# Where eight units of the shared expert run: ahead of the experts' loop, between the gate and table steps, in place of five

## The reference, cut to what matters

```
xf = layernorm(x)                                  # 2048 tokens x 512
scores = softmax(xf @ gate_w.T); topk_w, topk_idx = top_k(scores, 6)     # 64 experts
buf_tok[e, 0:128] = the first 128 tokens that chose expert e, in order   # buf_w: their weights
for each expert e:
    gu  = xf[buf_tok[e]] @ gate_up_proj[e]         # 128 x 512 @ 512 x 384
    hid = silu(gu[:, :192]) * gu[:, 192:]
    routed[buf_tok[e]] += (hid @ down_proj[e]) * buf_w[e]
shared = (silu(xf @ shared_gate_w.T) * (xf @ shared_up_w.T)) @ shared_down_w.T   # 384 wide
return x + routed + shared
```

## Time and profile before

| what | value |
|---|---|
| median of three runs | 596.72 us |
| the profiled execution: time, span | 597.44 us, 595.6 us |
| PE busy | 539.4 us, 91% of the span |
| DVE, ACT, POOL busy | 246.1, 161.7, 225.1 us |
| chain that ended last, by engine | PE 76%, DVE 11%, DMA 5%, issue 4% |
| its largest lines | L852 29%, L711 11%, L722 7%, L837 6% |
| mean granted TensorE clock | 0.974 |
| bytes moved | 155.05 MB, mean 260 GB/s |

### The profile page before, as it was taken

One profiled execution on the slowest core, in us unless ns is written; L12 is line 12 of the kernel. 1 busy time (PEld: TensorE's weight loads), 2 busy tenths in 40 slices (PEclk: granted clock), 3 DMA queues, 4 the chain that ended last, 5 costly groups with the idle time before them and its releaser, 6 DMA issues.

```text
span 595.6 us, 6264 instructions
## 1 busy us (share of the span) xinstructions
PE 539.4 (91%) x2087; PEld 291.8 (49%) x2087; DVE 246.1 (41%) x641; ACT 161.7 (27%) x342; POOL 225.1 (38%) x221
## 2 busy tenths in 40 slices
PE   5999996676799999999999999999999999999490
PEld 2555543343355555555555555555555555554130
DVE  1885979999223222222123223222222223223473
ACT  4767787662111111211111111212111111210000
POOL 3052246632523543444334543444344434412300
PEclk9999999987999999999999999999999999999796
DMA  8956478795458999899988999999999999785486
GB/s 288 338 208 235 113 255 278 245 390 205 124 198 276 298 298 298 289 305 280 278 271 267 295 327 306 281 267 292 268 289 307 295 291 288 180 249 119 51 316 255
DMA packets 53559, 155.05 MB, mean 260 GB/s; under 512 B 7248, under 2 KB 8784, under 8 KB 51856
## 3 DMA queue, kind: packets, MB, share of 16 engines
q1 hardware_dynamic: 34800, 109.74, 50.8%
q0 software_dynamic: 16320, 40.39, 29.6%
q10 hardware_dynamic: 2400, 4.46, 2.2%
HBM read 116.28 MB, written 38.28 MB: 260 GB/s over the span
## 4 chain that ended last, share of the span: by engine, by line
PE 76%; DVE 11%; DMA 5%; issue 4%; ACT 2%; POOL 1%; DVEq 0%; SPq 0%; POOLq 0%; ACTq 0%
PE bank L852 29%; PE bank L711 11%; PE bank L722 7%; PE bank L837 6%; PE bank L811 5%; PE bank L827 5%; PE bank L834 5%; PE bank L624 5%; DMA out<-y,table 3%; PE bank L612 2%; PE bank L818 2%; DVE x L1109 1%; DVE bn L1112 1%; DMA w<-in_W 1%; DVE ones_hi L1174 1%
## 5 line engine op out<-in xcount | busy, mean ns | idle before, releaser
L852 PE MATMUL bank<-gu_w,gxT 128*128 128x384 f32 x512 | 178.9, 493 | 2.2 <-ACT gxT L1040 1.4
L547 POOL DMA_INDIRECT out<-y,table x35 | 55.8, 1593 | 213.4 <-DVE y L1337 194.6
L852 PEld LDWEIGHTS bank<-gu_w,gxT 128*128 128x128 f32 x512 | 93.3, 190 | 79.7 <-issue 28.8
L1048 ACT ACTIVATE eg<-bank 128x192 f32<-128x192 f32 x64 | 21.2, 332 | 287.6 <-PE bank L852 284.6
L711 PE MATMUL bank<-xnT,upT 128*128 128x512 f32 x192 | 90.5, 617 | 8.5 <-DVE shid L1214 8.5
L1323 DVE TENSOR_TENSOR hid<-bank,eg 128x192 f32<-128x192 f32 x64 | 22.9, 358 | 179.7 <-ACT eg L1048 164.1
L553 POOL DMA_INDIRECT gx<-rows_dram,table x64 | 63.3, 989 | 28.2 <-issue 19.2
L1337 DVE TENSOR_SCALAR y<-bank,gx 128x512 f32<-128x512 f32 x64 | 45.1, 746 | 60.3 <-PE bank L837 60.3
L711 PEld LDWEIGHTS bank<-xnT,upT 128*128 128x128 f32 x192 | 36.3, 198 | 47.2 <-issue 37.9
L624 PE MATMUL bank<-w,h1T 128*128 128x512 f32 x128 | 57.7, 593 | 0.0
L547 POOL DMA_INDIRECT odd_sum<-y,table x29 | 45.9, 1584 | 8.9 <-issue 8.9
(11 more groups left out here) (179 smaller groups left out, 512.8 us busy)
## 6 DMA issues: line engine op xcount, KB each, us to landing
gu_w<-in_gate_up SPq DMA_DIRECT2D x64, 768.0 KB, 6.5
dn_w<-in_down SPq DMA_DIRECT2D x32, 768.0 KB
x<-in_x SPq DMA_DIRECT2D x4, 1024.0 KB, 13.0
feat_dram<-feat SPq DMA_DIRECT2D x16, 256.0 KB, 4.0
out<-shid SPq DMA_DIRECT2D x8, 512.0 KB
odd_sum<-shid SPq DMA_DIRECT2D x8, 512.0 KB
rows_dram<-rows ACTq DMA_DIRECT2D x4, 1024.0 KB, 6.4
gu_w<-out SPq DMA_DIRECT2D x4, 1024.0 KB, 7.9
```

The lines of the kernel that those rows point to most:

```text
L547: pool.indirect_dma_start(sums[lane(e)], bass.IndirectOffsetOnAxis(ap=table[:, e:e + 1], axis=0), y[:, e % YB, :], None, compute_op=ALU.ad ...
L852: last = nc.tensor.matmul(GU[e % 2][:, 0:2 * I], gxT[:, e % 2, c, :], gu_w[:, e % U, c, :], start=(c == 0), stop=(c == KC - 1))
```

## The change

`EARLY` goes from 5 to 8, so the loop holds 24 units in place of 27, spread over the same experts by the same formula. Ahead of the loop PE's order has units 0 to 5 each one place earlier or in a new place: unit 0 between the turns of tiles 5 and 6, unit 1 behind the logits of batch 1, unit 2 behind those of batch 2, unit 3 behind `invert_rest`, unit 4 between the last `place` and the third `invert`, unit 5 behind the first `collect`, and units 6 and 7 (the first two `shared_down`) behind the second. ACT's `silu` and DVE's `shared_up` steps move with them, and DVE adds the results of units 6 and 7 to `x` behind the last table step. One further line, in the general path that this execution doesn't enter, has another constant.

```diff
-EARLY = 5
+EARLY = 8
@@ PE
+                unit(0)
                 xn_turn(6)
                 xn_turn(7)
                 place(0)
                 gate(1)
                 turn_logits(1)
-                unit(0)
+                unit(1)
...
                 turn_logits(2)
-                unit(1)
+                unit(2)
                 invert(0)
...
                 invert_rest()
-                unit(2)
+                unit(3)
                 place(3)
+                unit(4)
                 invert(2)
                 pe.wait_ge(cross2_ready, 1)
                 collect(RFIN, cross2, k.pick_z, lambda lo_: lo_).then_inc(spare_done, 1)
-                unit(3)
+                unit(5)
                 invert(3)
                 pe.wait_ge(cross_ready, 1)
                 collect(LIST, cross, k.pick_a, lambda lo_: SLO - 1 - lo_).then_inc(fin_done, 1)
-                for u in range(4, EARLY):
+                for u in range(6, EARLY):
                     unit(u)
@@ ACT
                 gate_exp(1)
+                copy_logits(2)
                 silu(0, 0)
-                copy_logits(2)
                 store_rows(2)
...
                     copy_xn(3 * TB + t)
+                silu(0, 1)
                 gate_exp(2)
                 copy_logits(3)
                 store_rows(3)
                 gate_exp(3)
-                silu(0, 1)
@@ DVE
                 split_low(1)
+                shared_up(0, 0)
                 split_rest()
-                shared_up(0, 0)
                 choose(3)
...
                 cross_of(cross2, RTB, cross2_ready)
+                shared_up(0, 1)
                 split_high(3)
                 split_low(3)
                 dve.wait_ge(spare_done, 1)
                 nc.vector.tensor_copy(spare[:], POS[:, RFIN])
-                shared_up(0, 1)
+                shared_up(0, 2)
                 dve.wait_ge(tbl_done, B)
                 cross_of(cross, TBL, cross_ready)
...
                 link(nc.vector.tensor_tensor(gap[:], top[:, :, 0], top[:, :, 1], ALU.subtract))
+                for u in range(2 * SC, EARLY):
+                    shared_down(u - 2 * SC)
@@ general path
-            stage(vector=lambda: nc.vector.tensor_scalar(fits[:], bank[2][:, 0:E], SHI - 0.5, None, ALU.is_lt))
+            stage(vector=lambda: nc.vector.tensor_scalar(fits[:], bank[2][:, 0:E], SHI - 0.5 - AWAY, None, ALU.is_lt))
```

## The result

| | before | after |
|---|---|---|
| median (lowest to highest) of four runs each | 597.05 us (596.23 to 599.62) | 588.43 us (588.27 to 589.87) |
| the profiled execution: time, span | 597.44, 595.6 us | 588.57, 587.0 us |
| mean granted TensorE clock | 0.974 | 0.980 |
| PE busy | 539.4 us | 537.9 us |

The ratio is 0.9856, with a 95% interval of 0.983 to 0.9882: 8.6 us less, where 9.3 were forecast. PE's busy time hardly moves, since the units aren't fewer; they only stand where PE idled.

The account below looks back on a forecast made before the run. PE was taken to bound the loop, and DVE's tables the part ahead of it. Saving 8.6 us in the loop and 0.7 ahead gave 9.3 us off the 596.72 median: 587.4 us, range 585.8 to 591.0.

Parts of the forecast that it names:

- The loop follows PE: In the loop, a unit costs its full PE time, so moving three out saves 8.60 us (bounds 0 to 8.60).
- the loop isn't shorter: Rival, 7%: loads or scatters pace the loop, PE idles in the units' place, only 0.7 us stays: 596.0 us.
- my argument on the loads: In the loop, weights are asked for 23 us ahead and the slowest landing took 14.9 us, so loads keep up.
- Ahead of the loop: Before the loop, the last `invert` starts at 149.5 instead of 150.27: 0.7 us gained, bounds 0 and 0.8.
- The step on unit 5: Behind the first `collect`, unit 5 ends at 147.9 to 149.3, ahead of DVE's tables at 149.5, which alone hold `invert`.
- Unit 2: Behind batch 2's logits, waits for the silu ending near 118.1, ends at 121.6, before the first `invert` at 122.30; cost 0.
- the cover gone: Ahead of the first `invert`, without its idle time unit 2 would delay only turns that have slack of their own.
- Units 6 and 7: Behind the second `collect`, need 5.16 of the 5.2 us before the gather's rows: 0 if they fit, at worst 4.4 late.
- The clock rival: Rival, 12%: the clock falls just ahead of units 6 and 7, which end late: 589.0 to 590.5 us.
- its two prices: Units 6 and 7 end 3.1 us late (590.5 us) after a 6.8 us half-clock stretch, 1.6 late (589.0) after half that.
- The factor 1.85: Slowdown of a unit at the lower clock, from 6.35 us against 3.44 at the full clock, used in the late-end prices.
- everything from there on only moves earlier: From expert 58's scatter at 530.89 to the kernel's end, all steps only start earlier, so the loop's saving is kept.

Follow-up runs that it names:

- e7: Changed kernel with its 24 loop units packed one to an expert from expert 2 on, experts 26 to 63 having none: 593.22 us, ratio 0.992.
- e3: Changed kernel with two further `shared_down` (units 8 and 9) moved from the loop to behind the second `collect`: 588.88 us, ratio 0.9864.
- e5: Changed kernel with units 6 and 7 back in the loop and six matmuls whose results nobody reads in their place: 594.56 us, ratio 0.9953.
- e8: Changed kernel with DVE's last `shared_up` step, behind the loop, put ahead of the wait for the last scatters: 588.5 us, ratio 0.9843.
- e6: Changed kernel with ACT's first silu ahead of the copy of batch 2's logits again, as in the kernel before: 588.1 us, ratio 0.9836.
- e2: Changed kernel with units 6 and 7 back in the loop and units 0 to 5 left ahead of it: 596.14 us, ratio 0.998.
- e1: Changed kernel with units 5, 6 and 7 back in the loop, keeping the new order of units 0 to 4: 599.71 us, ratio 1.0042.

## Why the prediction was right, point by point

**The loop follows PE.** Forecast 8.60 us, measured 8.57, with the pairs at the forecast's lengths and PE's waits at 2.2 us. The rival "the loop isn't shorter" is out: even at 9.34 us for pair after pair PE waited for no load (e7). The Trainium skill's rule in the page "Perfetto Trace Analysis", section "Identifying the Most-Contended Engine", would have looked for room in PE's low share of weight loads; in e7's window that share is 6.90 of 12 us, and still the pairs took PE's own time. What my argument on the loads left out are the scatters. The rival named them, but only as something that PE would wait for; in e7 they fell behind while PE waited for none, and the price came behind the loop. The change doesn't reach that limit.

**Ahead of the loop.** Forecast 0.7 us (0 to 0.8), measured 0.24. The step on unit 5 held: the last `invert` waits for DVE alone. It started 0.42 us earlier, not 0.7 (149.85 against the chain's 150.27; in order of time the kernel before's `invert` stands at 150.10), and so missed the 149.6 that the prediction had given as a sign. The sum had left no room for an execution that ran late before that stretch, and this one did: DVE began to add the third batch's picked rows to `x` at 113.00 us, 1.05 later than in the kernel before's execution (111.95), and 0.24 of that was left at the end of its tables (149.79 against 149.55). Unit 0 didn't cause it, for PE's turn of the first batch's logits, ahead of it, was 1.13 us late already (91.43 against 90.30). With the same order up to there the last `invert` began at 148.89 in e3 and at 149.91 in e5; so this term, within a microsecond, is the execution's.

**Unit 2.** The text called it wrong if unit 2 held back an `invert` that DVE had made ready, and in the changed profile it did. It had the silu end near 118.1; it ended at 120.4, since the clock had fallen to 0.50 and batch 2's logits came late. Nor was this execution alone: with this order unit 2 held back the first `invert` in nine of ten profiled executions, and in all nine the clock had fallen between 112 and 118 us. In e8 it was at 1.00 there; the silu ended at 118.5, and the `invert` waited for DVE, as forecast. Why the clock falls there so often stays open. The cost is what the prediction gave for "the cover gone", nothing, and e6 shows it: with the silu first the wait is back on DVE and the time stays.

**Units 6 and 7** were to need 5.16 us of 5.2, and took 5.23. The chain now runs through them, so the place is full: the first turn comes 7.55 us after the last `invert` begins, and in e2, which has nothing there and waits for the gather, 7.50. e3 confirms it from the other side: two units more there bring nothing.

**The clock rival** was given 12%. It came in three of seven executions, and made the first turn 1.2 to 1.5 us late, counted from the last `invert`, near the smaller of its two prices (1.6 us). The factor 1.85 in these prices is somewhat small: the unit of the earlier trace rows ended at the full clock (granted 0.55 in 566 to 568 us, 1.00 in 568 to 570), while e1's first group, at 0.50 nearly to its end, took 5.44 us against 2.82, a factor 1.93. The median of 588.43 lies between the forecast's 587.4 and that price's 589.0. How often it came in the timed runs of the changed kernel itself can't be read from them. The idle time ahead of these units doesn't decide it, as the same idle time stood ahead of either outcome. The Trainium skill's page "TensorE: Matmul & The Clock Gate", section "What's actually happening", makes the low clock the state that an idle engine falls back to; that agrees with e2, where the granted clock was 1.00 up to 152 us, fell to 0.50 within 5.19 us of idle time, and the first group took 5.28 us.

**What the prediction didn't see** is why units must stand behind `collect` at all. It counted them as work that fits into a hole. That the same hole without them starts the loop at half clock, 2.9 to 3.1 us (e1, e2, e5), stands nowhere in it. It cost the forecast nothing, because the kernel before had a unit there as well and so the effect cancels; it cost me two expectations.

**The end.** Forecast "everything from there on only moves earlier". It did: expert 58's scatter starts 8.82 us earlier, against 522.07, and the part behind the loop differs by 0.2 us.

## What to carry to other kernels

Price a movable unit by comparing stretches of the loop with and without it: if the stretch grows by just the unit's length, the unit is worth all of its length in any hole elsewhere, until that hole is full. Look also at what the work in a hole does for what follows it: a hole right ahead of a matmul loop, left empty, gave back some 3 us at half clock here. And before filling or emptying a loop further, look at the chains that PE never waits for, such as scatters into one sum; they showed as a limit only behind the loop.

## What was not expected of the hardware

- After 5.2 us without a matmul the next group of eight ran 5.28 to 5.44 us in place of 2.82. Six matmuls whose results nobody reads, put into the gap, brought it back to 2.82 (e5).
- The clock is not decided by the program alone: the same idle times ahead of the same matmuls left it at 1.00 in one execution and at 0.50 in another (the windows of the changed kernel and of e8).
- One core moved 365 GB/s in a window of 12 us, gathers, scatters and weights mixed, at a share of 1.05, with PE busy all the time (e7). Loads landed in 9.1 us at the median instead of the 6.5 of the earlier trace rows, scatters in 8.1 instead of 7.2.
